# Six-stage decoder kernel: loads moved ahead of their stage, clears split between copies, narrow matmuls widened to 128 rows

## What is computed

```python
x = ln(x + L0_attn(x))          # 16 heads of 128, local window plus top-8 of 32 compressed keys, RoPE
x = ln(x + L0_xattn(x, ctx))    # 16 heads of 16, all 2048 context rows, fake-quantised q, k, v, probabilities
x = ln(x + L0_ffn(x))           # silu(x Wg) * (x Wu), 1024 wide, then Wd
x = ln(x + L1_attn(x))          # 32 heads of 8, causal
x = ln(x + L1_xattn(x, ctx))    # 16 heads of 16, against the sequence's own 128 context rows
x = ln(x + L1_ffn(x))           # 16 experts of 176, top 6 by router, plus a shared expert of 352
```

## Time and profile before

| | |
|---|---|
| median of 3 runs | 3405.3 us (3404.88 to 3410.69) |
| profiled execution: time, span | 3404.58 us, 3402.5 us |
| busy: PE, DVE, ACT, POOL | 2843.1, 2051.8, 1734.7, 331.7 us |
| mean granted TensorE clock | 0.951 |

### The profile page before, as it was taken

The page is one execution under the profiler, slowest core; times in us unless marked ns, Lnnn a source line. Parts: engine busy times, 40 slices in busy tenths (PEclk is TensorE's granted clock), DMA queues, the critical chain, the costliest instruction groups (busy, mean ns, idle before and its releaser), DMA issues. The chain is left out here.

```text
span 3402.5 us, 62151 instructions
## 1 busy us (share of the span) xinstructions
PE 2843.1 (84%) x20390; PEld 1830.9 (54%) x20564; DVE 2051.8 (60%) x4452; ACT 1734.7 (51%) x2944; POOL 331.7 (10%) x358
## 2 busy tenths in 40 slices
PE   3999999999575777777777789798948879999998
PEld 2777777777443555555555445455525545555554
DVE  4777777777388888888888622366626642323232
ACT  1555655655366999999999311266625531111010
POOL 1122121121400000000000000011112310000000
PEclk9999999999797999999999689899969989999999
DMA  4000000000000000000000100000050000000000
GB/s 160 1 0 0 0 0 0 0 0 0 13 22 0 0 0 0 0 0 0 0 0 0 40 0 0 13 0 0 0 148 11 9 2 0 0 0 0 0 0 25
DMA packets 34295, 38.13 MB, mean 11 GB/s; under 512 B 2949, under 2 KB 32449, under 8 KB 33217
## 3 DMA queue, kind: packets, MB, share of 16 engines
q10 hardware_dynamic: 17360, 19.22, 1.7%
q1 hardware_dynamic: 16880, 18.19, 1.7%
HBM read 35.29 MB, written 2.10 MB: 11 GB/s over the span
## 5 line engine op out<-in xcount | busy, mean ns | idle before, releaser
L1325 PE MATMUL x_p_s<-x_kT,x_qz 128*128 128x512 bf16 x897 | 283.3, 387 | 177.6 <-DVE f_wg L1407 120.5
L2314 DVE TENSOR_TENSOR f_h<-f_act_g,f_p_u 128x512 f32<-128x512 f32 (+1 forms) x132 | 90.7, 687 | 548.5 <-PE f_p_y L2209 480.5
L1407 DVE TENSOR_SCALAR_CACHE_REDUCE f_wg<-x_p_s,x_nsq 128x1024 f32<-128x1024 f32 x256 | 328.7, 1284 | 78.4 <-PE x_p_s L1325 64.5
L2259 ACT ACTIVATE f_act_g<-f_p_g 128x512 f32<-128x512 f32 (+1 forms) x132 | 78.4, 597 | 577.1 <-PE f_p_g L2194 577.0
L1407 DVE TENSOR_SCALAR_CACHE_REDUCE f_wu<-x_p_s,x_nsq 128x1024 f32<-128x1024 f32 x256 | 328.6, 1284 | 24.6 <-issue 23.1
L1384 ACT ACTIVATE x_ints<-f_wg,x_nb 128x2048 uint16<-128x2048 f32 x128 | 256.3, 2002 | 85.6 <-DVE x_nb L1428 85.6
L1334 PEld LDWEIGHTS x_p_t<-identb,x_ints 128*128 128x128 bf16 x4096 | 251.2, 98 | 64.5 <-ACT x_turned L1393 23.4
L2194 PE MATMUL f_p_g<-f_xT,f_wg 128*128 128x512 f32 (+1 forms) x528 | 271.1, 638 | 15.4 <-ACT f_xT L2246 10.1
L1334 PE MATMUL x_p_t<-identb,x_ints 128*128 128x128 bf16 x4096 | 272.6, 220 | 2.7 <-ACT x_turned L1393 2.7
L1384 ACT ACTIVATE x_ints<-f_wu,x_nb 128x2048 uint16<-128x2048 f32 x128 | 256.3, 2002 | 7.2 <-DVE x_nb L1428 0.8
L1393 ACT COPY x_turned<-x_p_t 128x1024 int32<-128x1024 int32 x256 | 253.9, 992 | 2.5 <-PE x_p_t L1334 2.5
(11 more groups left out here) (351 smaller groups left out, 5263.7 us busy)
## 6 DMA issues: line engine op xcount, KB each, us to landing
f_wg<-in_L_ffn_w_dram ACTq DMA_DIRECT2D x2, 1408.0 KB, 10.6
f_wu<-in_L_ffn_w_dram ACTq DMA_DIRECT2D x2, 1408.0 KB, 10.8
f_wd<-in_L_ffn_w_dram ACTq DMA_DIRECT2D x1, 2816.0 KB, 11.1
x_res<-in_x_dram SPq DMA_DIRECT2D x1, 2048.0 KB, 8.4
a_wq<-in_L_attn_Wq_dram ACTq DMA_DIRECT2D x1, 2048.0 KB, 7.6
a_wk<-in_L_attn_Wlk_dram ACTq DMA_DIRECT2D x1, 2048.0 KB, 12.0
a_wv<-in_L_attn_Wlv_dram ACTq DMA_DIRECT2D x1, 2048.0 KB, 16.3
a_wo<-in_L_attn_Wo_dram ACTq DMA_DIRECT2D x1, 2048.0 KB, 22.1
```

Source lines behind the costliest of these rows:

```text
L1325: mm = pe.matmul(p_s[half][:, c * BANK:(c + 1) * BANK], qz[:, par, :, :, :].rearrange("p a b t -> p (a b) t")[:, bass.ds(n, 1), :].rearran ...
L1407: dve.tensor_scalar(score[par][:, half, :], p_s[half][:, :], of_pass(nsq[:, par, :, :].rearrange("p a b -> p (a b)"), n), HIGHEST, ALU.mul ...
L2259: act.activation(act_g[n % 2][0:m, :], p_g[n % 2][0:m, :], ACT.Silu).then_inc(gate_up.sem, 1)
L2314: i = dve.tensor_tensor(h[n % 2][0:m, :], act_g[n % 2][0:m, :], p_u[n % 2][0:m, :], ALU.mult)
```

## The change

Three kinds of edit. (1) Loads: ACT issues the first attention's weights at once instead of after x, in the order q bias, Wq, k bias, Wlk, Wlv, Wk, Wv, Wo, each with a semaphore of its own that is waited for where the data is first used; eight tables move from the attention into `load_first`, and its constant `bias_o` from ahead of the pipeline into its second pass (`before=1` writes out one more pass of PE and ACT so that these waits stand in no loop). In the context attention the first context tile is loaded first. The loads of both small attentions are issued during the stage ahead. (2) POOL's clears of `qz` become 16, one after each copy of x. (3) `bias_rows`, `ones`, `spread` and `combT` get 128 rows, the new ones zero. One piece of POOL's order, the residual of the cross attention, comes a pass later.

```diff
-        self.bias_rows = sb("bias_rows", [3, BIAS_LEN], BF16)
-        self.ones = sb("ones", [3, P], BF16)
+        self.bias_rows = sb("bias_rows", [P, BIAS_LEN], BF16)
+        self.ones = sb("ones", [P, P], BF16)
...
             def _(act):
-                act.wait_ge(bias_in, 16 * len(BIASES))
-                act.wait_ge(loaded, 48)
                 ahead.load(act)
...
+            dve.memset(core.bias_rows[:, :], 0.0).then_inc(made, 1)
+            dve.memset(core.ones[:, :], 0.0).then_inc(made, 1)
+            dve.wait_ge(made, 7)
+            dve.memset(core.ones[0:3, :], 1.0)
...
+        for dst, src in self.tables:
+            eng.dma_start(dst, src).then_inc(self.tables_in, 16)
...
+        for j, name in enumerate(("L0_attn_Wq", "L0_attn_Wlk", "L0_attn_Wlv")):
+            if j < 2:
+                eng.dma_start(self.bias[j][:, :], A[("L0_attn_bq", "L0_attn_blk")[j]].partition_broadcast(P)).then_inc(self.bias_in[j], 16)
+            eng.dma_start(self.qkv[j][:, :, :], A[name].rearrange("(t p) n -> p t n", p=P)).then_inc(self.qkv_in[j], 16)
...
             def turn_in(b):
 
+                if isinstance(b, int) and b == 1:
+                    output_bias()
...
             ctx_in.open(sp)
+            sp.dma_start(cb[:, :], A["ctx_2048"][0, :, :]).then_inc(ctx_in.sem, 16)
+            sp.dma_start(wkv[:, :, :], A["L0_xattn_Wkv"].rearrange("(t p) n -> p t n", p=P)).then_inc(loaded, 16)
             sp.dma_start(wq[:, :, :], A["L0_xattn_Wq"].rearrange("(t p) n -> p t n", p=P)).then_inc(loaded, 16)
...
-            pool.memset(qz[XD * 4:P, 0, :, :, :].rearrange("p a b t -> p (a b t)"), 0.0).then_inc(zeroed, 1)
-            pool.wait_ge(zeroed, 1)
-            pool.memset(qz[0:XD * 4, 1, :, :, :].rearrange("p a b t -> p (a b t)"), 0.0).then_inc(zeroed, 1)
-            pool.wait_ge(zeroed, 2)
-            with pool.Fori(0, B) as b:
+            for b in range(B):
+                if b:
+                    pool.wait_ge(zeroed, b)
                 pool.wait_ge(turned.sem, turned.of(b - 1))
-                pool.tensor_copy(xb[:, :], core.x[:, bass.ds(b, 1), :].rearrange("p o h -> p (o h)")).then_inc(tile_in.sem, 1)
+                pool.tensor_copy(xb[:, :], core.x[:, b, :]).then_inc(tile_in.sem, 1)
+                pool.wait_ge(tile_in.sem, tile_in.of(b))
+
+                rows, par = ((slice(XD * 4, P), 0), (slice(0, XD * 4), 1))[b % 2]
+                pool.memset(qz[rows, par, b // 2, :, :].rearrange("p b t -> p (b t)"), 0.0).then_inc(zeroed, 1)
...
-            act.wait_ge(zeroed, 2)
...
+            if later:
+                later.load(sp)
+            sp.wait_ge(weights.loaded, weights.all_in)
...
+            for following in later:
+                following.load(sp)
...
-            spread = sb("spread", [64, tiles, P], BF16)
+            spread = sb("spread", [P, tiles, P], BF16)
...
-            combT = sb("combT", [64, NT], BF16)
+            combT = sb("combT", [P, NT], BF16)
```

More of the change, by code:

```diff
@@ L78, in end, with pipeline @@
         assert self.n == self.per, f"{self.n} links in a pass, {self.per} counted"
-def pipeline(eng, order, pieces, passes):
+def pipeline(eng, order, pieces, passes, before=0):
     depth = max(lag for _, lag in order)
+    first = depth + before
     def emit(i, there):
@@ L89, in emit @@
                 pieces[name](i - lag)
-    for i in range(depth):
+    for i in range(first):
         emit(i, lambda lag, i=i: lag <= i)
-    with eng.Fori(depth, passes) as i:
+    with eng.Fori(first, passes) as i:
         emit(i, lambda lag: True)
@@ L173, in _ @@
                 ahead.load_first(sp)
-            sp.wait_ge(made, 5)
+            sp.wait_ge(made, 6)
             for j in range(3):
@@ L429, in _, with output_bias @@
             pe.wait_ge(tables, TABLES)
[L432 to L436 removed]
+            def output_bias():
+                pe.wait_ge(weights.o_in, 16)
+                pe.matmul(p_o[:, 0:H], core.ones[:, :], core.bias("L0_attn_bo"), start=True, stop=False)
+                for h in range(NH):
+                    mm = pe.matmul(p_o[:, 0:H], kT[:, h, :], w_o[:, h, :], start=False, stop=(h == NH - 1))
+                mm.then_inc(bias_made, 1)
             def turn_in(b):
+                if isinstance(b, int) and b == 1:
+                    output_bias()
                 pe.wait_ge(tile_in.sem, tile_in.of(b))
@@ L1585, in small_attention @@
+def small_attention(core, tag, weights, orders, source=None, ahead=None, later=None):
     nc, A = core.nc, core.A
-    dk = H // heads
-    cross = bool(source)
+    heads, dk, cross = weights.heads, weights.dk, weights.cross
+    w, w_o, owner = weights.w, weights.o, weights.owner
+    if cross:
+        gains, bias_qk, bias_out, bias_v = weights.gains, weights.bias_qk, weights.bias_out, weights.bias_v
     per_row = ROWS // dk
@@ L2089, in load, with feed_forward @@
             eng.dma_start(dst, src).then_inc(self.loaded, 16)
-def feed_forward(core, tag, weights, experts):
+def feed_forward(core, tag, weights, experts, later=()):
     nc, A = core.nc, core.A
@@ L2422, in constants, with program @@
     return c
-def program(nc, A, out, stop=6, start=0):
+def program(nc, A, out):
     with ExitStack() as ctx:
```

197 lines of the change are left out of this document (102 added, 95 removed).

## The result

Over four runs of each the changed kernel takes 3365.6 us (3361.7 to 3374.1) against 3408.0 (3404.9 to 3414.4) for the kernel before: a ratio of 0.9877, 95% interval 0.9852 to 0.9901, so 42 us faster (1.2%). Forecast were 3339 and a range of 3314 to 3370. The profiled execution took 3374.1, the longest of the four, with a span of 3372.4 and a mean granted clock of 0.948.

A forecast was written before the change was run, and what follows sets the result against it. It took TensorE to bound first attention and experts, DVE's chain the context operands, and stage starts to count in full. Terms −29.7 − 4.8 − 21 − 2 − 3.5 − 5.5 = −66.5 gave 3339 us, range 3314 to 3370.

The forecast's parts named there:

- `spread` and `combT`, −29.7: Experts' feed-forward: 128 rows avoid about 0.30 us lost at each of 100 64-row matmuls, −29.7 us.
- Bias rows, −4.8: First attention: 16 widened bias matmuls save 0.3 us each, −4.8 (0 to −6); context attention nothing or some tenths.
- Start of the context operands, −25: Context operands: with the copy before the clears, projection starts at about 906.1 instead of 930.68, −25 us.
- Clears, +4 taken from 0 to +22: Context operands: 16 clears between copies delay DVE by 0.25 us per pass, +4; bounds 0 and +22.
- The nearest row: Context operands: a DVE instruction beside POOL's copy took 0.54 instead of 0.43 us, basis for +0.25 per pass.
- the clears stop DVE: Rival, context operands: each clear holds DVE for its remaining 1.45 us, +22 instead of +4, about 3357; chance 0.12.
- x, +8.5 taken from +6.4 to +20: First attention's head: x lands later beside 8.4 MB of weights, +8.5 us; up to 20 with all weights ahead.
- wrong in kind: Signs: experts' tile period staying 5.68, clock falling in a PE-bound stage, or first attention beginning later than 58.
- weights go ahead of x: Rival, first attention's head: x's 1 KB pieces lose to 8 KB ones, 20 us late, +11.5, about 3350; chance 0.08.
- The constant, +8: First attention: the constant's 17 matmuls now stand in PE's full second pass, +8 us (6.9 to 9.5).
- The small attentions, −9: Loads issued a stage ahead: self attention −3.5 us, cross attention −5.5 (0 to −12).
- PE's clock as the slower rival: Denser matmul stream makes the throttle grant 1.2 GHz for part of the experts' stage, 3412 or more; chance 0.04.

The follow-up runs named there:

- pad_f1: Kernel before with 128 rows in `spread` and `combT` alone (experts' stage): ratio 0.9901, −34 us.
- pad_bias: Kernel before with 128 rows in `bias_rows` and `ones` alone: ratio 0.9986, −5 us.
- the two experiments: Changed kernel with POOL's clears written as float32 (0.9818, −62 us), and changed kernel with ACT doing the clears instead of POOL (0.9809, −65 us).
- pad_only: Kernel before with 128 rows in all four tensors (`bias_rows`, `ones`, `spread`, `combT`) and nothing else: ratio 0.9874, −43 us.
- w_1k: Changed kernel with Wq, Wlk and Wlv each loaded in 8 pieces, 1 KB contiguous instead of 8 KB: ratio 0.9849, −51 us against the kernel before.
- x_first: Changed kernel with x issued by ACT ahead of the weights instead of by SP beside them: ratio 0.9856, −49 us against the kernel before.

## Why the prediction was right or wrong

The direction, and that the median lies in the range, rest on the padding: without its −43 the rest of the change is worth about nothing. The point was 27 us too low. The forecast of the profiled execution was 3338 and it took 3374.1, 36 more; by the table's lines 12.4 of that lie before the first turn, 9.1 in the first attention, 12.7 in the stretch with the clears, 4.0 in the experts' stage, and the others take back 2.

- **`spread` and `combT`, −29.7.** Right: 0.30 a tile to the hundredth. By itself it is worth −34; the 25.7 of the table are of a profile with a clock of 0.96 in that stage against 0.97 before, and in `pad_f1`'s profile the same stretch is 32.2 shorter.
- **Bias rows, −4.8.** The size is right (−5), the place wrong. The step that failed is "In the first attention PE is full, so 16 of them give 16 × 0.3": each pass is shorter by 0.30, but passes at a lower granted clock took it back but for 0.2 in twelve. And "beside DVE's chain and give nothing" failed too: DVE stood idle for 0.29 us a pass before it reads the projection of q, and stands for 0.10 in `pad_bias`; a pass of 6.07 instead of 6.32 makes 3.8 in 15, and the stretch is 4.1 shorter. That PE's bias matmul was in that chain is read from the two traces, and no run has tested it by itself.
- **Start of the context operands, −25.** Right, −25.3.
- **Clears, +4 taken from 0 to +22.** Mis-sized: 20.9 in the profiles (+16.7 with the bias rows' −4.2 in the same stretch), 20 to 23 by the two experiments. The passes of 7.7 that the prediction named as the sign of it came. The step that failed is "The nearest row": it was a two-input operation beside a copy, and the instructions that meet the clear are of another kind. The rival "the clears stop DVE" was the truth, and had 0.12; the rule of the page that the prediction set beside it was put aside for one row of the wrong kind.
- **x, +8.5 taken from +6.4 to +20.** Mis-sized: 28.7 − 8.4 = +20.3, and with it the first turn, at 60.5, passed the 58 beyond which the prediction called itself wrong in kind. "Nearer to equal shares, since x's transfer is the first one under way" failed: it wasn't the first, and its pieces were an eighth of the others'. The rival "weights go ahead of x" was the truth, and had 0.08. What was missed beyond it is that small transfers behind x starve as well, and that a barrier waits for them.
- **The constant, +8.** 8.3 in its pass (60.65 against 52.34). Right in the pass; the pass ahead of it is 2.8 longer too, so by the whole stretch, 855.1 against 844.1, it is 11. And the earlier first turn (−10) that was to pay for it never came: the stretch up to the context operands is 14.7 longer instead of 6.8 shorter.
- **The small attentions, −9.** Right: −7.4 in the two stretches, −8 by experiment and −10 by its profile.
- **PE's clock as the slower rival.** It didn't decide, but slow stretches exist on a small scale: in the first attention they took back nearly all that the padding saves there.

The misses at the clears and at x were priced as rivals, at +18 and +11.5, each taken for unlikely and never for both at once. With the table's 12.7 and 11.8 added to 3339 one comes to 3363.5, within 2 us of the median; that is partly luck, since it leaves out the 9.1 of the first attention, and the profile from which the two are read took 8.6 us more than the median.

## What to carry to other kernels

Before a load is moved ahead, list every small transfer that some barrier or first instruction still waits for. Here 2 MB in pieces of 1 KB took 28.7 us beside a queue of 8 KB pieces and 8.4 alone, bias rows of 3 KB issued from 9.9 on landed at 33, and an issue behind x was held for 19.44. Cutting a long clear on GpSimd into pieces moved it off a stage's start (−25), but onto DVE's casts and scalar operations (+21). ACT did the same clears with no loss in the pass (6.07 us, as in `pad_only`), and half as many elements of twice the width on GpSimd cost 0.2 a pass instead of 1.6. In a stream that PE bounds, give every matmul the same row count, by zero rows if need be; it was worth 0.30 us at each change of rows, 34 us in the experts' stage, while in the first attention slower passes took the gain back.

## What the runs showed that was not expected

- A matmul of 3 or 64 rows between matmuls of 128 costs 0.30 us, a third each ahead of it, behind it, and in the group after.
- SP's issue of a small load took 19.44 us while the queue ahead of it was starved, where 2.16 was the longest of a single one in setup before. In `w_1k` it took 7.49, and in `x_first`, with x on the other queue, 0.45: it is the issue right behind x that is held.
- The clear of 2048 bfloat16 over 64 rows took 1.80 us, and 2.09 where it began during a cast of DVE's (L1270, from 960.19): the stop goes both ways.
- The first attention's passes come in two lengths, 50.50 and 52.17 us (50.80 and 52.46 without padded bias rows), with a few of 53.85. Twelve of them add up to 614.4 or 617.8 with padding and to 614.6 or 618.0 without, though padding takes 0.30 off each.
